# A two-layer decoder on one core: expert stage in pairs of 128-row tiles and three blocks, four gathers in flight, last norm of stage one on ScalarE

## What is computed

```python
def _L1_ffn_ref(x, gate_w, gate_b, w1, b1, w2, b2):
    ...
    scores = xf @ gate_w + gate_b
    topk_s, topk_i = jax.lax.top_k(scores, TOP_K)
    comb = jnp.zeros_like(scores).at[jnp.arange(n)[:, None], topk_i].add(topk_s)
    h = jnp.maximum(jnp.einsum('nd,edh->neh', xf, w1) + b1, 0.0)
    eo = jnp.einsum('neh,ehd->ned', h, w2) + b2
    out = jnp.einsum('ne,ned->nd', comb, eo)
```

## Time and profile before

| | us |
|---|---|
| three runs | 2864.74, 2872.43, 2880.53 |
| median | 2872.43 |
| the profiled execution, its own time | 2876.24 |
| its span in the trace | 2874.5 |

### The profile page before, as it was taken

One profiled execution on the slowest core, in us unless ns is written; L12 is line 12 of the kernel. 1 busy time (PEld: TensorE's weight loads), 2 busy tenths in 40 slices (PEclk: granted clock), 3 DMA queues, 4 the chain that ended last, 5 costly groups with the idle time before them and its releaser, 6 DMA issues. The chain is left out here.

```text
span 2874.5 us, 49242 instructions
## 1 busy us (share of the span) xinstructions
PE 2397.5 (83%) x16164; PEld 1881.5 (65%) x16164; DVE 1971.9 (69%) x4760; ACT 1444.4 (50%) x2778; POOL 1335.4 (46%) x1248
## 2 busy tenths in 40 slices
PE   5888888579999579999999999878999885998670
PEld 3666666469999546566565665547888774997560
DVE  4888888556565357878888888745777775765563
ACT  3666666345555247777777777753444341222110
POOL 5777777544443255444344454403656553002545
PEclk9999999889999878999999999889999997999885
DMA  2222212152121000001000010003333343444665
GB/s 69 59 74 59 74 60 63 47 153 95 63 84 40 25 18 30 27 30 31 30 30 30 27 34 23 23 25 127 103 115 117 111 147 118 140 140 152 205 199 157
DMA packets 208168, 226.68 MB, mean 79 GB/s; under 512 B 32254, under 2 KB 194048, under 8 KB 207664
## 3 DMA queue, kind: packets, MB, share of 16 engines
q1 hardware_dynamic: 186352, 177.14, 19.7%
q0 software_dynamic: 20480, 46.39, 5.1%
q10 hardware_dynamic: 1088, 0.00, 0.0%
HBM read 131.99 MB, written 95.49 MB: 79 GB/s over the span
## 5 line engine op out<-in xcount | busy, mean ns | idle before, releaser
L1333 POOL TENSOR_TENSOR f_hm<-f_hm,f_mhalf 128x64 f32<-128x64 f32 x32 | 347.4, 10856 | 2.7
L1513 DVE TENSOR_REDUCE f_nm<-f_raw 128x4 f32<-128x1024 f32 x256 | 312.1, 1219 | 34.0 <-PE f_raw L1634 33.9
L1406 ACT ACTIVATE f_PT<-f_sco 128x1024 f32<-128x1024 f32 x256 | 262.7, 1026 | 81.7 <-PE f_sco L1652 78.7
L2359 POOL DMA_INDIRECT d_pick<-expert_out,e_out_slots x128 | 129.5, 1012 | 319.0 <-DMA expert_out<-d_eo 227.7
L2378 ACT ACTIVATE d_hh<-d_H 128x512 fp32r<-128x512 f32 x78 | 46.7, 598 | 283.9 <-PE d_H L2455 240.7
L1634 PE MATMUL f_raw<-f_k4T,f_q4T 64*128 64x256 f32 x1024 | 140.3, 355 | 37.5 <-DVE f_nm L1513 36.6
L895 ACT ACTIVATE b_hT<-b_H,b_b1r 128x512 f32<-128x512 f32 x128 | 88.3, 690 | 163.5 <-PE b_H L1024 148.5
L1634 PEld LDWEIGHTS f_raw<-f_k4T,f_q4T 64*128 64x128 f32 x1024 | 84.2, 203 | 105.8 <-DVE f_nm L1513 54.3
L1889 POOL DMA_INDIRECT expert_in<-g_xm,e_slots x128 | 130.9, 1023 | 39.7 <-issue 37.0
L1039 PE MATMUL b_O<-b_w2l,b_hTh 128*128 128x256 f32 x512 | 145.8, 285 | 0.0
L1039 PE MATMUL b_O<-b_w2h,b_hTh 128*128 128x256 f32 x512 | 144.8, 283 | 0.0
(11 more groups left out here) (364 smaller groups left out, 7755.6 us busy)
## 6 DMA issues: line engine op xcount, KB each, us to landing
d_xs<-expert_in SPq DMA_DIRECT2D x78, 256.0 KB
expert_out<-d_eo SPq DMA_DIRECT2D x78, 256.0 KB
x_scratch<-a_x SPq DMA_DIRECT2D x64, 256.0 KB, 2.2
b_w<-in_L_ffn_W_dram SPq DMA_DIRECT2D x16, 1024.0 KB
a_x<-in_x_dram SPq DMA_DIRECT2D x32, 256.0 KB
a_cx<-in_ctx_dram SPq DMA_DIRECT2D x32, 256.0 KB
f_x<-x_scratch SPq DMA_DIRECT2D x32, 256.0 KB
f_xr<-x_scratch SPq DMA_DIRECT2D x32, 256.0 KB
```

The lines of the kernel that those rows point to most:

```text
L1333: g.tensor_tensor(hm[b % 2][:, :], hm[b % 2][:, :], mhalf[:, :], ALU.pow).then_inc(hroot, 1)
L1406: s.activation(PT[n % 3][:, t, :, :], heads(SCO), ACT.Exp, scale=float(DH) ** -0.5).then_inc(probs_ready, 1)
L1513: v.tensor_reduce(nm[:, t, g * HG:(g + 1) * HG], heads(RAW), AX.X, ALU.max, negate=True)\
L2359: g.indirect_dma_start(pick[b % GR][:, t, c, :], None, ex.eo_d[k], bass.IndirectOffsetOnAxis(ap=ex.out_slots[:, b, t, c:c + 1], axis=0), b ...
```

## The change

1. Stage one: `norm4` and `passed_by` run on ScalarE, as x2 times a scale plus a bias; `root4` makes the scales and the bias for both, in five steps instead of two. `ORDER` is changed.
2. The attention stage's `ORDER` is changed.
3. Three blocks of 16, 10 and 6 batches; tiles of 128 rows, two to a pair, each with an expert of its own. Tiles per block are 72, 48 and 32, so 76 pairs.
4. The expert stage works on pairs. Loads are one per 128-row tile; the additions of b1 and b2 are two of 256 columns each; a tile's number is loaded into a register once and held for both uses, earlier in the queue (`hold`).
5. The ring of gathers holds four batches instead of three, and batches are merged from four pairs after their block's end on, every 1.5 pairs (so after pairs 40, 41, 43, 44, ...). The two last batches of block two fall on the end, with the six of block three.

```diff
 # stage one
-            "in stats", "in norm", "x2 kv", "route logits", "sco scores", "x2 sums", "x2 add", "ln sq", "in T",
-            "x2 stats", "sco exp", "route ranks", "in qk0", "ln scale", "sco prT", "in qk1", "ln kT", "x2 norm",
-            "sco inv", "sco att", "x2 T", "sco stats", "in v", "ln qT")
+            "in stats", "x2 kv", "route logits", "in norm", "sco scores", "x2 sums", "x2 add", "ln sq", "in T",
+            "x2 stats", "sco exp", "route ranks", "in qk0", "ln scale", "sco prT", "ln kT", "in qk1", "x2 norm",
+            "sco inv", "sco att", "ln qT", "x2 T", "sco stats", "x2 pass", "in v")
...
             def root4(b):
                 pool.wait_ge(var4, b + 1)
-                root(rs4[b % 2][:, :], mv4[b % 2][:, :, 1], T, None, rstd4)
-
-            def passed_by(b):
-                pool.wait_ge(x2n_ready, b + 1)
-                if b >= 3:
-                    pool.wait_ge(x3_stored[b % 3], 16 * (b // 3))
-                g.tensor_tensor(x3[b % 3][:, :, :], x2[b % 3][:, :, :], x2n[b % 2][:, :, :], ALU.add).then_inc(x3_ready, 1)
+                if b >= 2:
+                    pool.wait_ge(x3_ready, b - 1)
+                stand_alone(pool, pool_passed)
+                step(g.tensor_scalar(minus4[:, :], mv4[b % 2][:, :, 0], -1.0, None, ALU.mult))
+                step(g.tensor_scalar(rs4[b % 2][:, :], mv4[b % 2][:, :, 1], EPS, None, ALU.add))
+                step(g.tensor_tensor(rs4[b % 2][:, :], rs4[b % 2][:, :], mhalf[:, 0:T], ALU.pow))
+                step(g.tensor_tensor(nmr4[b % 2][:, :], minus4[:, :], rs4[b % 2][:, :], ALU.mult))
+                g.tensor_scalar(rsp4[b % 2][:, :], rs4[b % 2][:, :], 1.0, None, ALU.add).then_inc(rstd4, 1)
...
+            def norm4(b):
+                act.wait_ge(rstd4, b + 1)
+                if b >= 2:
+                    wait_full(act, "x2 T", b - 2)
+                for t in range(T):
+                    last = s.activation(x2n[b % 2][:, t, :], x2[b % 3][:, t, :], ACT.Identity,
+                                        bias=nmr4[b % 2][:, t:t + 1], scale=rs4[b % 2][:, t:t + 1])
+                last.then_inc(x2n_ready, 1)
...
 # dispatch
-        self.BLOCKS = (B - B // 3, B // 3)
-        self.NE, self.TILE = NE, 2 * P
+        self.BLOCKS = (B // 2, B // 2 - B // 5, B // 5)
+        self.NE, self.TILE, self.PAD = NE, P, 2 * P
...
-        self.tiles = [2 * n * S // self.TILE + NE - 1 for n in self.BLOCKS]
+        self.tiles = [2 * ((2 * n * S // self.TILE + NE) // 2) for n in self.BLOCKS]
 # attention
-            "in stats", "raw 0", "qk scale", "att 0", "raw 1", "att 1", "out o0", "in norm", "out o1", "raw 2",
-            "att 2", "head var", "in normT", "qk gamma", "out oT", "raw 3", "att 3", "in qk0", "qk high", "in qk1",
-            "out proj", "raw max0", "raw 4", "qk low", "att 4", "raw shift0", "in v", "raw 5", "qk split0", "att 5",
-            "qk split1", "qk split2", "raw 6", "qk split3", "att 6", "qk split4", "qk split5", "raw 7", "qk split7",
-            "att 7", "raw max1", "qk split6", "raw shift1", "att end")
+            "raw 0", "in stats", "att 0", "raw 1", "att 1", "out o0", "in norm", "out o1", "raw 2", "att 2",
+            "qk scale", "head var", "in normT", "qk gamma", "out oT", "att 3", "raw 3", "in qk0", "qk high",
+            "in qk1", "out proj", "raw max0", "raw 4", "qk low", "att 4", "raw shift0", "raw 5", "in v", "qk split0",
+            "att 5", "qk split1", "qk split2", "raw 6", "qk split3", "att 6", "qk split4", "qk split5", "att 7",
+            "raw 7", "raw max1", "qk split7", "qk split6", "raw shift1", "att end")
 # expert stage
-    XR, ER, GR = 6, 3, 3
+    XR, ER, GR = 6, 3, 4
...
-                if k + 1 < len(ex.BLOCKS):
-                    ready_after.append(first[k + 1] + 2 + b * (ex.tiles[k + 1] - 3) // n)
-                else:
-                    ready_after.append(N)
+                after = ready_after[-1] + 1.5 if ready_after else 0
+                ready_after.append(min(N, max(after, sum(pairs[:k + 1]) + 4)))
+        ready_after = [int(m) for m in ready_after]
...
             for m in range(N):
                 h_low(m)
+                hold(m + 1, 0)
                 if m + 2 < N:
                     x_low(m + 2)
+                hold(m + 1, 1)
                 if m + 1 < N:
                     add_b1(m + 1)
```

More of the change, by code:

```diff
@@ L444, in square_ctx, with passed_by @@
                 s.activation(kv[b % 2][:, :, :], cx[b % CR][:, :, :], ACT.Square).then_inc(kv_ready, 1)
+            def norm4(b):
[6 more added lines that the diff above has]
+                last.then_inc(x2n_ready, 1)
+            def passed_by(b):
+                act.wait_ge(rstd4, b + 1)
+                if b >= 3:
+                    act.wait_ge(x3_stored[b % 3], 16 * (b // 3))
+                for t in range(T):
+                    last = s.activation(x3[b % 3][:, t, :], x2[b % 3][:, t, :], ACT.Identity,
+                                        bias=nmr4[b % 2][:, t:t + 1], scale=rsp4[b % 2][:, t:t + 1])
+                last.then_inc(x3_ready, 1)
             def take_x2nT(b):
@@ L2252, in experts_phase @@
     NE = ex.NE
-    C, T = D // P, ex.TILE // P
+    C, T = D // P, 2
     B = sum(ex.BLOCKS)
     ROWS = ex.xs_d.shape[0]
-    TILES = [(k, j) for k, n in enumerate(ex.tiles) for j in range(n)]
-    N = len(TILES)
-    XR, ER, GR = 6, 3, 3
+    PAIRS = [(k, j) for k, n in enumerate(ex.tiles) for j in range(0, n, T)]
+    N = len(PAIRS)
+    XR, ER, GR = 6, 3, 4
     with ExitStack() as ctx:
@@ L2289, in experts_phase @@
         x5_rows, out_rows = rows(ex.x5_d), rows(out.rearrange("b s d -> (b s) d"))
-        first = [sum(ex.tiles[:k]) for k in range(len(ex.tiles))]
+        pairs = [n // T for n in ex.tiles]
         ready_after = []
@@ L2349, in _ @@
             for k, n in enumerate(ex.BLOCKS):
-                done = first[k] + ex.tiles[k]
+                done = sum(pairs[:k + 1])
                 for r in range(ER):
@@ L2401, in add_b1 @@
                     dve.wait_ge(hT_psum, m - 1)
-                v.tensor_tensor(up_sb[m % 2][:, :, :], halves(UB[m % 2]),
-                                b1[:, bass.ds(e, 1), :].broadcast_to([P, T, D]), ALU.add).then_inc(up_ready, 1)
+                for t in range(T):
+                    e = held[m, t]
+                    last = v.tensor_tensor(up_sb[m % 2][:, t, :], halves(UB[m % 2])[:, t, :],
+                                           b1[:, bass.ds(e, 1), :].rearrange("p o d -> p (o d)"), ALU.add)
+                last.then_inc(up_ready, 1)
             def h_low(m):
@@ L2415, in add_b2 @@
                     dve.wait_ge(eo_stored[m % ER], 16 * (m // ER))
-                v.tensor_tensor(eo[m % ER][:, :, :], halves(OB[m % 2]),
-                                b2[:, bass.ds(e, 1), :].broadcast_to([P, T, D]), ALU.add).then_inc(eo_ready, 1)
+                for t in range(T):
+                    e = held[m, t]
+                    last = v.tensor_tensor(eo[m % ER][:, t, :], halves(OB[m % 2])[:, t, :],
+                                           b2[:, bass.ds(e, 1), :].rearrange("p o d -> p (o d)"), ALU.add)
+                last.then_inc(eo_ready, 1)
             def merge(b):
@@ L2434, in _ @@
             x_low(1)
+            hold(0, 0)
+            hold(0, 1)
             add_b1(0)
@@ L2469, in hT, with hold, product @@
                 transposes(HB[m % 2], up_sb[m % 2]).then_inc(hT_psum, 1)
-            def product(bank, high, low, n, e):
+            held = {}
+            def hold(m, t):
+                if m < N:
+                    k, j = PAIRS[m]
+                    held[m, t] = pe.value_load(ex.expert[k][0:1, j + t:j + t + 1], min_val=0, max_val=NE - 1)
+            def product(bank, high, low, n, m):
                 for t in range(T):
+                    e = held[m, t]
                     for c in range(C):
@@ L2495, in down @@
                     pe.wait_ge(eo_ready, m - 1)
-                product(OB[m % 2], hh[m % 2], hl[m % 2], 1, e).then_inc(out_psum, 1)
+                product(OB[m % 2], hh[m % 2], hl[m % 2], 1, m).then_inc(out_psum, 1)
             pe.wait_ge(consts, 2)
+            for m, t in ((0, 0), (0, 1), (1, 1)):
+                hold(m, t)
             xT(0)
```

57 lines of the change are left out of this document (26 added, 31 removed).

## The result

The changed kernel takes **2895.21 us** (median of 7 runs, 2890.73 to 2904.21) where the kernel before takes 2872.03 in the same comparison. The ratio is **1.0089, 95% interval 1.0068 to 1.0111**: slower by 0.9%, 23 us, where 84 us less had been forecast. The profiled execution has a span of 2900.2 us against 2874.5.

What follows compares the result with a forecast made beforehand. DVE's in-order queue was taken to set stage one's round, PE the plain expert tiles. Terms -28 - 8 + 8 + 1 - 36 - 21 = -84 us gave 2788 us against the 2872.43 median; range 2725 to 2850.

Steps and rivals of the forecast that it cites:

- Stage one, 15.0 us a round: Stage one: rounds fall from 15.94 to 15.0 us, 0.95 over 30 full rounds, -28 us.
- rival five: Stage one: ScalarE's queue becomes the bound, 17.9 us a round, +64, stalls at old price, 2916 us; chance 0.06.
- Rival three: Stage one: the x2 addition, parted from POOL's residual addition, loses 1.1 us more a round, 2755 us; chance 0.06.
- Attention, -0.25 us a round: Attention stage: the new order takes 0.25 us off each of 32 rounds, -8 us.
- Cross, +8: Cross stage: a third block's table made by DVE mid-round adds 8 us, between 6.5 and 10.
- A pair is PE's 3.81 us as before, since every product stays: Expert stage: pairs stay at 3.81 us, so 76 pairs against 78 tiles give -7.6 us.
- A few tenths there cost nothing: Expert stage: DVE's halved additions and moved register loads cost nothing while PE bounds.
- The stall about half as often, 2.4 us a merge: Expert stage merges: 2.4 us each instead of 3.9, 24 merges giving -28, with two pairs fewer -36 us.
- Rival one: Expert stage: gathers without pause still stop DVE, 24 merges at 3.9 us, +8 instead of -28, 2824 us; chance 0.26.
- Rival two: Expert stage: stalls were the register load's exposed wait, now covered, 1.05 us a merge, 2755 us; chance 0.14.
- End, -21: End, after the last tile: 24 gathers instead of 40, at 1.32 us apart, -21 us.
- the signs of being wrong that were set: Stage one over 520 us, attention over 1000 or under 960, DVE waits before b1's addition over 60 us or none.

Runs made afterwards that it cites:

- the first group: The runs e1 to e4, all on one chip, where the kernel before takes 2814.04 us.
- e2: Changed kernel, PE's products of both tiles of a pair using the first tile's expert weights: 2776.14 us, ratio 0.9858.
- e3: Changed kernel, POOL gathering for the first four batches only, later merges reading what these left: 2770.06 us in one run.
- e4: Changed kernel with a pause on POOL (memset of 128x1024) after each batch's four gathers: 2790.75 us, ratio 0.9908.
- e1: Kernel before with only the change's stage one (norm and ORDER) and attention ORDER: 2789.4 us, ratio 0.9907.
- e13: Same kernel as e2 (changed kernel, first tile's expert for both tiles), on another chip: 2888.88 us, ratio 1.0055.
- e7: Changed kernel with one of DVE's two register loads moved later, behind x_low: 2903.48 us, ratio 1.0116.
- e10: Same kernel as e1 (kernel before with the change's early stages), on another chip: 2848.07 us, ratio 0.9904.
- e8: Same kernel as e4 (changed kernel with POOL's pause), on a chip that stalls: 2839.18 us, ratio 0.9878.
- e11: Kernel before with the change's early stages plus a pause on POOL after each batch's gathers of the first block: 2829.12 us, ratio 0.9853.
- e14: Same as e11 but with a shorter pause (memset of 128x64, about 1 us): 2831.9 us, ratio 0.9848.

## Why the prediction was wrong

- *Stage one, 15.0 us a round*: right, 15.07. The total was -16 and not -28: the 29 full intervals between takes of x2nT give 24.1 us, the last two, in rounds without new batches, take back 6.0 (they are 13.66 and 12.68 us where they were 10.69 and 9.63), and the first take comes 2.0 us later. The sum counted 30 rounds and no ends. One round after, PE's two stops, DVE's addition of x2, the two additions of the residual on POOL, and the norm on ScalarE:

```profile
305.13 0.63 PE L652 MATMUL a_bank<-a_ident,a_xn 128*128 128x128 f32 x4 [0.26 <-DVE a_xn L493]
...
306.53 1.96 PE L677 MATMUL a_bank<-a_w,a_xnT 128*128 128x512 f32 x4 [0.67 <-ACT a_xnT L394]
```

```profile
306.45 2.67 DVE L562 SCALAR_TENSOR_TENSOR a_x<-a_prod,a_rs,a_x 128x256 f32<-128x256 f32 x2
```

```profile
306.17 1.27 POOL L335 TENSOR_TENSOR a_res<-a_x,a_xn 128x512 f32<-128x512 f32 x1
307.51 1.33 POOL L336 TENSOR_TENSOR a_res<-a_res,a_bv 128x512 f32<-128x512 f32 x1
```

```profile
312.42 1.10 ACT L453 ACTIVATE a_x2n<-a_x,a_nmr,a_rs 128x256 f32<-128x256 f32 x2 [1.33 <-POOL a_rsp L365]
```

  PE stops 0.93 us in place of the 1.74 of the earlier trace rows. Both stops belong to the first norm's way to the projections; the one of 0.5 to 0.7 us that I had put at kT isn't there. ScalarE does wait for the late root, 1.33 us, but PE has other work then, so **rival five** fell. (Its +64 is 59 for 30 rounds of 17.9 us, which changes nothing.)
- *Rival three* (the x2 addition runs free) fell: it takes 2.67 us, more than the 2.04 of the earlier trace rows, and ends at 309.12, 0.28 us after the residual. That is the exclusion of the Trainium skill (SBUF — State Buffer, SBUF: two separate sides), and the trace agrees with it again; the new order made the two meet for longer: the addition now starts 1.0 us before the first of POOL's two ends.
- *Attention, -0.25 us a round*: of the right sign, and near in total, partly by luck. Takes of xnT are 797.4 us apart, first to last, for 811.9, -0.47 a round, nearly twice the forecast; 3.5 us come back behind the last, which the sum had no term for. PE's idle time ahead of the raw scores, where the gain was looked for, fell from the 37.5 us of the earlier trace rows to 33.2, under a third of the 14.5 us between first and last take:

```profile
L1649 PE MATMUL f_raw<-f_k4T,f_q4T 64*128 64x256 f32 x1024 | 131.6, 338 | 33.2 <-DVE f_nm L1528 30.4
```

- *Cross, +8*: half of what it cost, +20.4 with the start (forecast +9). The third table is there as forecast (rounds of 22.73 and 21.34 us, against one of 21.55):

```profile
2148.14 0.60 ACT L1962 ACTIVATE g_xmT<-g_bank 128x512 f32<-128x512 f32 x1 [5.15 <-PE g_bank L2168]
2170.87 0.60 ACT L1962 ACTIVATE g_xmT<-g_bank 128x512 f32<-128x512 f32 x1 [12.27 <-PE g_bank L2168]
```

  The other 29 rounds came to 9 us more than before as well. Part of the 20, up to half, goes with the chip: on that of the first group the stretch takes 464.5 us in e2, e3 and e4 and 453.7 in e1, +11, near the forecast; on the others it takes 472 to 475 with three blocks and 452 to 460 with two. Two rounds that take 16.5 us on the chips that stall are among it; they take 12.9 and 13.1 on that chip. From the first to the last take the granted clock is 0.94 against 0.97 before. What makes the rest, the padding or something else, wasn't tried.
- ***A pair is PE's 3.81 us as before, since every product stays***: the first step that failed. The products stayed, but the register operations that PE's queue works through between them doubled, and the sum put them at nothing. Every second pair is held up behind a register load of 0.5 to 0.6 us; 4.22 us a pair on average, 15 us in all by e13, which keeps 0.12 us a pair over 3.81 that isn't explained. "A few tenths there cost nothing" for DVE's loads failed too: in e7 moving one costs 0.2 us a pair.
- ***The stall about half as often, 2.4 us a merge***: the step that decided. The 39 pairs took 280.5 - 39 x 3.81 = 132 us over the plain price, 5.5 a merge, where 58 were forecast and 86 stood before. At the 4.22 us that a plain pair now takes, 116 of them are left, 4.8 a merge. I had seen that the stalls go with gathers without a pause, and put them in DVE and at its register load. They are PE's results that arrive late: ScalarE, which loads no register, is held up as well. And I had counted on the pairs of merges to leave pauses: a spacing of 1, 2, 1, 2 pairs empties two ring places within 5 us, so POOL gathers eight times in a row in every cycle of three pairs. The stall did not become rarer but regular. Each stops PE for about 6 us. The granted clock of the 3.2 us after such a stop is 0.50, the lower level of 1.2 GHz, with products 0.21 us apart in place of 0.12, which is 1 to 2 us more (the whole stretch's mean is 0.83):

```profile
2649.60:2652.80 3.20, 3.20 (x15) 3.20 (x16) 1.86 (x4) 1.20 (x2) 0.00 (x0) 0.50 0.34 114
```

  The reading of the earlier trace rows was also a little off: the batch that ends at 2675.45 started 0.73 us after the end of the one before it, where 0.30 is the usual distance, and the stall came all the same.
- *Rival one* (the stalls stay) was right that they go with gathers without a pause, wrong on whose they are, and too low in its price: 3.9 us a merge would have given 2824. *Rival two* (the stalls were the register load) fell by the longest load of DVE, 0.96 us beside waits of 3 to 6, by ScalarE's wait, and by e7, whose stalls are as long. A register load takes about 600 ns at least by the Trainium skill (DMA: Bandwidth & Descriptors, Latency and other measured facts), an estimate of 1.2 us for two exposed ones. The trace does not agree, and it decides: e7 shows 0.2 us a pair for moving one back, and the median of the queue's own record of the load is half the page's figure:

```profile
L2415 DVEq TENSOR_LOAD <-e_expert x152: 297/314/962, 2418.4 to 2851.0; - x152
```

- *End, -21*: right, -21.1.
- Of the signs of being wrong that were set, two came: stage one is over 520 us (527 by the stretch), and DVE's waits before the addition of b1 beside merges are over 60 (54.5 us in twelve of the misnamed waits alone, and 29 more marked "issue").

Put together, the 25.7 us between the two spans are, on the chips that stall: early stages -27 us (25 by the medians of e1 and e10), end -21, two tiles fewer -8, cross +20, PE's address arithmetic +15, and the rest of the expert stage some +46. Nearly all of that is the stalls: against the first group's chip they cost 49 us with the old expert stage (26 intervals in 178 us in e10, 129 in e1) and 99 with the new one (280.5 us, 181 in e4). e8's pause gives back 63 us of the stretch. Not settled is why PE's results are late beside gathers (the matmul's end is modelled, and nothing here tells a late result from a late signal of it), and why on some chips only: of the four chips of the experiments one doesn't show it (whether the chip of the first comparison is one of the other three isn't known), with the same instructions and the same 1.30 us between gathers. Taking single gathers apart, or moving them to another queue, wasn't tried.

The fastest kernel on the chips that stall is e11, or e14 within the noise: the early stages of the change, the old expert stage and a pause after each batch's gathers, 2829 us against 2872. Neither was run on the chip that doesn't stall; there e1 and e4, both about 2790 us, are the fastest that compute the whole result.

## What to carry to other kernels

Where a product's operand is addressed by a register, count the register operations a tile before and after, and look at the queue's register loads too: here the operations doubled with the finer choice of expert, and 15 us were paid in the queue of an engine that had no slack. Spread indirect transfers evenly, try a pause behind every few of them, and look at what a stop is waiting for on the producer's side: the end of the matmul against the start of its reader shows a late result, whatever name stands in the bracket. Time a candidate on more than one chip before a difference of one per cent is believed: here the same kernel differed by 2% between chips.

## What the runs showed of the hardware

- Beside eight gathers in a row, results of PE reached ScalarE and DVE 4.8 and 7.8 us after the last matmul's end; ScalarE's own result passed on at once (d_xh ends at 2644.89, d_xl starts at 2644.92). On the chip of the first group no delay over 0.8 us is seen beside 88 gathers in a row.
- That chip runs the kernel before 58 us faster than the others. For one and the same kernel, e1 there and e10 on a chip that stalls, 49 of the 63.5 us between the traces lie beside merges (129 and 178 us for 26 intervals), the rest in the attention and cross stages.
- With PE's stops shortened by a pause on another engine, the granted clock of the stretch was 0.98 of the full 2.4 GHz in place of 0.83.
- A load of a register from SBUF by PE's queue took 0.30 us in the median, and up to 0.63 in the changed kernel; all 16 loads over 0.45 us ahead of the gathers overlapped one of DVE's, but 15 short ones did too.
